# Longer turns on TensorE: sixteen pairs of sums, then half a batch of weighing

## The chip, the cores and the metric

The kernel runs on one core of a Trainium2 chip. The metric is the device time of one execution in microseconds (us); several executions are made and their median is taken. A core has engines that run side by side and wait for each other through semaphores: TensorE (PE in the profile, with its weight loads as PEld), VectorE (DVE), ScalarE (ACT), GpSimd (POOL, idle here) and SyncE (SP), which issues the transfers. TensorE writes only into PSUM, eight banks of 512 words in each of 128 partitions; ScalarE and VectorE bring results from there into the working memory, which the kernel holds as one large tensor called `arena`.

## The reference

The input `r_x` has 512 samples of 39 fields of 64 numbers. Two layers are computed, each a weighted sum over products of pairs of fields, and both are summed over the last axis:

```
h = x                               # (512, 39, 64)
for W in (W0, W1):                  # (39, 39, 128), (39, 128, 128)
    h = einsum('bid,bjd,ijh->bhd', x, h, W)
    outs.append(h)
y = concatenate(outs, axis=1).sum(axis=-1)      # (512, 256)
```

## The kernel before

The kernel doesn't build the first layer for each sample. It folds W0 and W1 into one table of coefficients, `c0`, with 115 slots of 128 columns, and then needs for each sample only sums over the 64 numbers of products of fields. The program has three stretches.

In the first two (TensorE at L381 and L402, ScalarE at L340, VectorE at L325) the table is made. In the third, from about 103 us to the end, the samples go through. They come in **pairs** (two samples in two halves of the partitions, 256 pairs in all), four pairs make a **group**, two groups a **unit**, and four units, that is eight groups, a **batch** of 32 pairs. There are eight batches.

In this stretch each engine has its own loop in a fixed order:

- VectorE makes the products of fields for a unit (`products`, L282 to L295) into a ring of four units, once TensorE is done with the unit that lay there (semaphore `filled`).
- TensorE makes the sums of a group in `sums` (L425): 16 matmuls with a stationary operand of 64x32 and 230 columns. Eight of them, on two halves of the rows and four strips of 32 columns, can be in the array together. Since the numbers are fp32, each matmul stands in the trace as two passes, so that a group has 32 and a unit 64. A group fills a **couple** of PSUM banks. There are three couples, taken in turn (`couple(g)` is `g % 3` after the first batch), and `sums` waits on the semaphore `emptied` until the group that last used its couple has been copied out.
- ScalarE copies a group out of its couple with four copies (L360) into the sums of the batch, `s0`, of which there are two, and then counts `emptied` up.
- TensorE weighs a batch in `weigh` (L446): 115 matmuls, one for each slot, with the 64 sums of the slot as stationary operand and 128 columns of the table moving. They go in pairs on the two halves of the columns. The last part also has eleven matmuls at L454 and four at L460, and then `batch_done` is counted up. Weighing of a batch is spread over the sums of the batch that follows. The last batch is weighed by itself at the end.
- ScalarE takes a weighed batch out of PSUM at L347, before the first group of a later batch; VectorE adds its halves at L302. SyncE loads the fields (L205), moves four rows of sums across partitions when a batch has been copied out (`gather`, L241), and stores results (L246).

The four units of the first batch are summed amid the second stretch; 28 units remain for the loop on TensorE that the change rewrites:

```
for u in range(BATCH_UNITS, UNITS):
    n, turn = divmod(u, BATCH_UNITS)
    sums(2 * u)
    sums(2 * u + 1)
    weigh(n - 1, turn)
```

Here `weigh(n, turn)` does the slots from `each * turn`, with `each` 29: a quarter of the table's 115.

Of the kernel before, what the change touches and what calls it, by code (L numbers as in the profile page):

```python
# [21 lines left out]
SLOTS = 115  # L22
# [60 lines left out]
def cin_kernel(nc: bass.Bass, x: bass.AP, u_list: bass.AP, w1: bass.AP, v_first: bass.AP, v_second: bass.AP,  # L83
# [9 lines left out]
    BATCH_UNITS = PAIRS // UNIT  # L93
    UNITS = ALL_PAIRS // UNIT
    GROUPS = ALL_PAIRS // GROUP
    BATCH_GROUPS = PAIRS // GROUP
# [9 lines left out]
    IN_BANK = BANK // HID  # L106
    MIXED = (SLOTS + IN_BANK - 1) // IN_BANK
    CROSS = COPY1

    ctx = ExitStack()  # L110
    with ctx:
# [7 lines left out]
        def take(words):  # L119
            at = used[0]  # L120
            used[0] += words
            assert used[0] <= WORDS
            return at
# [12 lines left out]
        w0_t2_0 = take(4 * HID)  # L136
        c1_x0 = take(CROSS * HID)
        t2_0 = take(2 * 4 * B)
# [8 lines left out]
        c1_x_second0 = w0_t2_second0 + 4 * HID  # L147
        assert c1_x_second0 + CROSS * HID <= s0[1]
        w1_0 = s0[1]
# [33 lines left out]
        def mixed_bank(k):  # L183
            return k if k < 8 else k % 4
# [18 lines left out]
        def _(sp):  # L203
# [22 lines left out]
            sp.dma_start(view(w0_t2_second0, (1, 4 * HID)), w0_t2[1]).then_inc(out1_loaded, 16)  # L226
            sp.dma_start(view(c1_x0, (1, CROSS * HID)), c1_x[0]).then_inc(out1_loaded, 16)
            sp.dma_start(view(c1_x_second0, (1, CROSS * HID)), c1_x[1]).then_inc(out1_loaded, 16)
            for u in range(BATCH_UNITS, X_RING):
# [33 lines left out]
        def _(dve):  # L263
# [44 lines left out]
            dve.wait_ge(out1_loaded, 64)  # L308
            for at, second, words in ((w0_t2_0, w0_t2_second0, 4 * HID), (c1_x0, c1_x_second0, CROSS * HID)):
                w = view(at, (1, words))  # L310
# [58 lines left out]
        @block.tensor  # L369
        def _(pe):  # L370
            for i in range(DIRECT):
                if i >= 4:
                    pe.wait_ge(direct_copied, i - 3)
                for k in range(8 * i, 8 * i + 8):
                    piece, at = divmod(k, PIECE)
                    if at == 0:
                        pe.wait_ge(w1_loaded[piece], 16)
                    for c in range(4):
                        if k == 0 and c < 2:
                            pe.wait_ge(u_ready, c + 1)  # L380
                        done = nc.tensor.matmul(  # L381
                            bank_view((i % 4 * 2 + k % 8 // 4) * BANK + k % 4, (4, SLOTS),
                                      rows=(ROWS * c, ROWS * c + ROWS)),
                            view(w1_0 + piece * PLACES * PIECE + ROW0[c % 2] * PIECE + at, (PIECE, ROWS)),
                            view(u0 + c % 2 * LIST + c // 2 * SLOTS, (1, SLOTS)), start=True, stop=True)
                done.then_inc(direct_filled, 1)

            def mixed(k):
                bank = mixed_bank(k)
                if k < 8:  # L390
                    pe.wait_ge(direct_copied, DIRECT - 4 + k // 2 + 1)
                else:
                    pe.wait_ge(c_added, k - 8 + 1 if k < 12 else k - 4 + 1)
                first = [True] * 4
                for j in range(IN_BANK * k, min(IN_BANK * k + IN_BANK, SLOTS)):
                    of = [terms(c % 2, PAIR_OF[c][j]) for c in range(4)]
                    for t in range(2):
                        for c in range(4):
                            if t >= len(of[c]):
                                continue  # L400
                            row, m = of[c][t]
                            done = nc.tensor.matmul(  # L402
                                bank_view(bank * BANK + j % IN_BANK * HID, (1, HID), rows=(ROWS * c, ROWS * c + ROWS)),
                                view(v0 + row * ROWS, (1, ROWS)), view(w1_0 + m * PIECE, (PLACES * PIECE, PIECES), (1, PIECE)),
                                start=first[c], stop=True, skip_group_check=True)
                            first[c] = False
                done.then_inc(mixed_filled, 1)

            def sums(g):
                u, turn = divmod(g, 2)  # L410
                before = last_user(g)
                if before is not None:
                    pe.wait_ge(emptied, before + 1)
                else:
                    pe.wait_ge(c_added, COUPLES[couple(g)] + 2 if g < BATCH_GROUPS else MIXED)
                if turn == 0:
                    pe.wait_ge(prod_ready, u + 1)
                for m in range(2):
                    for odd in range(2):
                        pair = GROUP * turn + 2 * odd + m  # L420
                        for r in range(2):
                            rows = (HALF * r, HALF * r + HALF)
                            for which in range(2):
                                c = 2 * odd + which
                                done = nc.tensor.matmul(  # L425
                                    bank_view((COUPLES[couple(g)] + r) * BANK + m, (2, LIST),
                                              rows=(ROWS * c, ROWS * c + ROWS)),
                                    view(x0 + u % X_RING * XU + pair * X_WORDS + X_MAIN + ROW0[which], (1, ROWS), rows=rows),
                                    view(prod0 + u % PROD_RING * PROD + pair * 2 * LIST + which * LIST, (1, LIST), rows=rows),
                                    start=True, stop=True)  # L430
                done.then_inc(filled, 1)

            def weigh(n, turn):
                at = (2 + n % 2) * BANK
                if turn == 0:
                    pe.wait_ge(emptied, BATCH_GROUPS * (n + 1))
                    if n == 0:
                        pe.wait_ge(c_added, MIXED)
                    if n >= 2:
                        pe.wait_ge(out_ready, n - 1)  # L440
                each = -(-SLOTS // BATCH_UNITS)
                for j in range(each * turn, min(each * turn + each, SLOTS)):
                    side = j % 2
                    rows = (HALF * side, HALF * side + HALF)
                    sums_of = view(s0[n % 2] + j * B, (1, B))
                    nc.tensor.matmul(bank_view(at + HID, (1, HID), rows=rows), sums_of, view(c0 + j * HID, (1, HID)),  # L446
                                     start=j < 2, stop=True, skip_group_check=True)
                if turn < BATCH_UNITS - 1:
                    return
                if n == 0:  # L450
                    pe.wait_ge(out1_ready, 2)
                for j in range(CROSS):
                    side = j % 2
                    nc.tensor.matmul(bank_view(at, (1, HID), rows=(HALF * side, HALF * side + HALF)),  # L454
                                     view(s0[n % 2] + j * B, (1, B)), view(c1_x0 + j * HID, (1, HID)),
                                     start=False, stop=True, skip_group_check=True)
                pe.wait_ge(t2_moved[n % 2], 64 * (n // 2 + 1))
                for c in range(4):
                    side = 1 - c % 2
                    done = nc.tensor.matmul(bank_view(at, (1, HID), rows=(HALF * side, HALF * side + HALF)),  # L460
                                            view(t2_0 + (4 * (n % 2) + c) * B, (1, B), rows=(0, SLOTS)),
                                            view(w0_t2_0 + c * HID, (1, HID), rows=(0, SLOTS)),
                                            start=False, stop=True, skip_group_check=True)
                done.then_inc(batch_done, 1)

            pe.wait_ge(v_ready, 1)
            for k in range(MIXED):
                mixed(k)
                if k in SUMS_BEHIND:
                    sums(2 * SUMS_BEHIND[k])  # L470
                    sums(2 * SUMS_BEHIND[k] + 1)
            for u in range(BATCH_UNITS, UNITS):
                n, turn = divmod(u, BATCH_UNITS)
                sums(2 * u)
                sums(2 * u + 1)
                weigh(n - 1, turn)
            for turn in range(BATCH_UNITS):
                weigh(BATCHES - 1, turn)


# [90 lines left out]
```

## Time and profile before

| | |
|---|---|
| median of three runs | 275.45 us (273.75 to 276.93) |
| profiled execution | 277.26 us, of which its span 275.5 us |
| granted TensorE clock over the span | 0.994 |
| TensorE busy | 258.4 us (94%) |
| VectorE, ScalarE busy | 173.6 us, 156.3 us |

The span goes from the first instruction to the last; the execution's own time has 1.8 us more around it. A TensorE record is a pass of a matmul, with an end that is modelled, so the distance from start to start tells more than the length of one. A weight load (PEld) belongs to each pass. "L425" is line 425 of the kernel as printed above. In a row of the timeline, brackets say how long the engine was idle before it and what released it; "issue" means that the profile shows nothing it waited for.

### The profile page before, as it was taken

The page shows a single profiled execution, that of the slowest core. Times are in us where ns is not written, and L with a number is a line of the kernel's source. Part 1 is how long each engine was busy: PE and PEld are TensorE (multiplying, and loading weights), DVE is VectorE, ACT ScalarE, POOL GpSimd, SP SyncE. Part 2 cuts the span into 40 slices and gives each one's busy share as a digit, 9 for nine tenths or more (in the row PEclk, how much of TensorE's full clock was granted, in tenths as well). Part 3 has the DMA queues.
Part 4 walks back from the last instruction along what each step waited for, and adds up shares of the span by engine and source line. Part 5 has one row for each costly group of instructions (what it writes and reads, how often), then busy time and mean ns, then how long its engine had stood idle before and what let it go on. Part 6 is the DMA issues. An engine that isn't in the chain of part 4 may idle for free.

```text
span 275.5 us, 14507 instructions
## 1 busy us (share of the span) xinstructions
PE 258.4 (94%) x6842; PEld 232.8 (85%) x6842; DVE 173.6 (63%) x333; ACT 156.3 (57%) x281; POOL 0.2 (0%) x4
## 2 busy tenths in 40 slices
PE   0977789999999999999999999999999999999995
PEld 0967789998999978888888888888888888888994
DVE  1009996733397699996887986996898689200000
ACT  1242344004164267887787887877887788778300
POOL 0000000000000000000000000000000000000000
PEclk9997999999999999999999999999999999999999
DMA  6999200001011012222132222322231220100100
GB/s 220 356 406 413 82 2 5 6 5 49 5 51 45 11 52 66 68 79 66 51 91 67 63 61 62 98 59 58 66 99 50 69 58 2 29 5 2 29 2 10
DMA packets 11019, 20.78 MB, mean 75 GB/s; under 512 B 4816, under 2 KB 5584, under 8 KB 10704
## 3 DMA queue, kind: packets, MB, share of 16 engines
q1 hardware_dynamic: 10960, 19.87, 23.3%
q8 instruction: 53, 0.87, 1.3%
q14 instruction: 6, 0.05, 0.1%
HBM read 18.40 MB, written 0.52 MB: 69 GB/s over the span
## 4 chain that ended last, share of the span: by engine, by line
PE 94%; issue 2%; DMA 2%; DVE 0%; SPq 0%; ACT 0%
PE psum L446 39%; PE psum L425 20%; PE psum L402 18%; PE psum L381 12%; PE psum L454 3%; DMA arena<-in_w 2%; PE psum L460 2%; SPq L213 0%; DVE arena L325 0%; DVE arena L302 0%; ACT arena L347 0%
## 5 line engine op out<-in xcount | busy, mean ns | idle before, releaser
L360 ACT COPY arena<-psum 64x460 f32<-64x460 f32 x256 | 137.3, 536 | 63.2 <-PE psum L425 60.1
L446 PEld LDWEIGHTS psum<-arena 128*64 128x64 f32 x1840 | 102.3, 137 | 10.3 <-issue 10.3
L446 PE MATMUL psum<-arena 128*64 128x128 f32 x1840 | 109.3, 274 | 0.0
L284 DVE TENSOR_TENSOR arena<-arena 128x1600 f32<-128x1600 f32 x32 | 58.2, 1820 | 0.1
L425 PE MATMUL psum<-arena 64*32 64x230 f32 x2048 | 57.5, 357 | 0.7 <-DVE arena L325 0.7
L402 PE MATMUL psum<-arena 128*32 128x128 f32 x1690 | 50.5, 274 | 0.2
L402 PEld LDWEIGHTS psum<-arena 128*32 128x32 f32 x1690 | 48.2, 109 | 2.7 <-issue 2.7
L425 PEld LDWEIGHTS psum<-arena 64*32 64x32 f32 x2048 | 38.1, 106 | 11.7 <-issue 5.6
L381 PE MATMUL psum<-arena 128*32 128x115 f32 x1024 | 32.3, 289 | 13.0 <-DMA arena<-in_w 6.9
L381 PEld LDWEIGHTS psum<-arena 128*32 128x32 f32 x1024 | 30.6, 163 | 14.5 <-issue 7.6
L325 DVE TENSOR_TENSOR arena<-arena,psum 128x512 f32<-128x512 f32 (+1 forms) x29 | 19.3, 682 | 21.2 <-PE psum L402 21.1
L295 DVE TENSOR_TENSOR arena<-arena 128x800 f32<-128x800 f32 x32 | 31.6, 988 | 0.0
L340 ACT COPY arena<-psum 128x920 f32<-128x920 f32 x16 | 14.8, 926 | 29.4 <-PE psum L381 29.4
L293 DVE TENSOR_TENSOR arena<-arena 128x720 f32<-128x720 f32 x32 | 29.0, 905 | 0.0
L302 DVE TENSOR_TENSOR arena<-psum,arena 64x256 f32<-64x256 f32 x8 | 3.3, 412 | 36.4 <-ACT arena L347 36.4
L282 DVE COPY arena<-arena 128x72 f32<-128x72 f32 x32 | 6.3, 198 | 19.3 <-PE psum L425 19.3
L347 ACT COPY arena<-psum 64x256 f32<-64x256 f32 x8 | 2.9, 368 | 23.0 <-PE psum L460 23.0
L273 DVE TENSOR_TENSOR arena<-arena 128x3040 f32<-128x3040 f32 x1 | 3.3, 3326 | 16.3 <-DMA arena<-in_v_second 16.3
L454 PE MATMUL psum<-arena 128*64 128x128 f32 x176 | 12.0, 273 | 0.0
L454 PEld LDWEIGHTS psum<-arena 128*64 128x64 f32 x176 | 10.9, 137 | 0.0
L289 DVE TENSOR_TENSOR arena<-arena 128x128 f32<-128x128 f32 x32 | 9.2, 287 | 0.0
L287 DVE TENSOR_TENSOR arena<-arena 128x128 f32<-128x128 f32 x32 | 9.2, 287 | 0.0
(13 smaller groups left out, 41.8 us busy)
## 6 DMA issues: line engine op xcount, KB each, us to landing
arena<-in_x SPq DMA_DIRECT2D x32, 312.0 KB, 3.2
arena<-in_w SPq DMA_DIRECT2D x4, 640.0 KB, 5.7
arena<-in_v_first SPq DMA_DIRECT2D x1, 1520.0 KB, 8.8
arena<-in_v_second SPq DMA_DIRECT2D x1, 1520.0 KB, 12.1
arena<-in_c_x SPq DMA_DIRECT2D x2, 704.0 KB, 11.4
arena<-arena SPq DMA_DIRECT2D x32, 28.8 KB
arena<-in_w_t SPq DMA_DIRECT2D x2, 256.0 KB, 8.9
out<-arena SPq DMA_DIRECT2D x8, 64.0 KB, 2.8
```

The source lines that it names most:

```text
L284: mult(view(to + 20, TO, (10, 20), (1, 10)), view(main, T, (1, 20), (0, 10)), view(x, T, (1, 20), (1, 10)), ALU.mult)
L287: mult(view(to, TO, (8, 2), (1, 8)), view(x + X_N1, T, (0, 2), (1, 8)), view(x + X_N1, T, (2, 2), (1, 8)), ALU.mult)
L293: mult(view(second + 25, TO, (10, 9), (1, 10)), view(half, T, (1, 9), (0, 10)), view(half, T, (1, 9), (1, 10)), ALU.mult)
L295: mult(view(second + 130, TO, (10, 10), (1, 10)), view(half + 9, T, (1, 10), (0, 10)), view(half + 9, T, (1, 10), (1, 10)), ALU.mult).then ...
L325: add(c, c, bank_view(mixed_bank(k) * BANK, (1, words)), ALU.add).then_inc(c_added, 1)
L340: nc.scalar.copy(view(c0 + 8 * i, (4, 2), (HID, SLOTS), (1, 4)), bank_view(i % 4 * 2 * BANK, (BANK, 2), (4, SLOTS), (1, 4))).then_inc(dire ...
L360: done = nc.scalar.copy(view(s0[n % 2] + 8 * in_batch + 4 * odd, (B, SLOTS), (2, 2), (1, 2), rows=(HALF * q, HALF * q + HALF)), bank_view( ...
L381: done = nc.tensor.matmul(bank_view((i % 4 * 2 + k % 8 // 4) * BANK + k % 4, (4, SLOTS), rows=(ROWS * c, ROWS * c + ROWS)), view(w1_0 + pi ...
L402: done = nc.tensor.matmul(bank_view(bank * BANK + j % IN_BANK * HID, (1, HID), rows=(ROWS * c, ROWS * c + ROWS)), view(v0 + row * ROWS, (1 ...
L425: done = nc.tensor.matmul(bank_view((COUPLES[couple(g)] + r) * BANK + m, (2, LIST), rows=(ROWS * c, ROWS * c + ROWS)), view(x0 + u % X_RIN ...
L446: nc.tensor.matmul(bank_view(at + HID, (1, HID), rows=rows), sums_of, view(c0 + j * HID, (1, HID)), start=j < 2, stop=True, skip_group_che ...
L454: nc.tensor.matmul(bank_view(at, (1, HID), rows=(HALF * side, HALF * side + HALF)), view(s0[n % 2] + j * B, (1, B)), view(c1_x0 + j * HID, ...
```

## The change

The loop over units becomes a loop over groups. After every fourth group, in place of every second, a part of the weighing follows, and the parts are halves (`TURNS` is 2, `each` becomes 58) in place of quarters. Every matmul, copy, product and transfer remains, with the same semaphores; only TensorE's order changes. The other engines' programs are the same.

```
+    TURN = 4
+    TURNS = BATCH_GROUPS // TURN
...
-                each = -(-SLOTS // BATCH_UNITS)
+                each = -(-SLOTS // TURNS)
...
-                if turn < BATCH_UNITS - 1:
+                if turn < TURNS - 1:
                     return
...
-            for u in range(BATCH_UNITS, UNITS):
-                n, turn = divmod(u, BATCH_UNITS)
-                sums(2 * u)
-                sums(2 * u + 1)
-                weigh(n - 1, turn)
-            for turn in range(BATCH_UNITS):
+            for g in range(BATCH_GROUPS, GROUPS):
+                n, in_batch = divmod(g, BATCH_GROUPS)
+                sums(g)
+                if in_batch % TURN == TURN - 1:
+                    weigh(n - 1, in_batch // TURN)
+            for turn in range(TURNS):
                 weigh(BATCHES - 1, turn)
```

TensorE's order at the start of the third stretch, before. One group is a row with its waits and the row of fifteen behind it; L446 is the weighing.

```order
L425 MATMUL psum<-arena 32x230 [waits prod_ready,c_added]
L425 MATMUL psum<-arena 32x230 x15
L425 MATMUL psum<-arena 32x230 [waits emptied]
L425 MATMUL psum<-arena 32x230 x15
L446 MATMUL psum<-arena 64x128 [waits c_added,emptied]
L446 MATMUL psum<-arena 64x128 x28
L425 MATMUL psum<-arena 32x230 [waits prod_ready,emptied]
```

Two groups, 29 weighings, and the next groups. The same place after the change, where line 425 has become 427 and 446 has become 448:

```order
L427 MATMUL psum<-arena 32x230 [waits prod_ready,c_added]
L427 MATMUL psum<-arena 32x230 x15
L427 MATMUL psum<-arena 32x230 [waits emptied]
L427 MATMUL psum<-arena 32x230 x15
L427 MATMUL psum<-arena 32x230 [waits prod_ready,emptied]
L427 MATMUL psum<-arena 32x230 x15
L427 MATMUL psum<-arena 32x230 [waits emptied]
L427 MATMUL psum<-arena 32x230 x15
L448 MATMUL psum<-arena 64x128 [waits c_added,emptied]
L448 MATMUL psum<-arena 64x128 x57
```

The third and fourth group moved ahead of the first weighing. With three couples the fourth group waits for the copies of the first, and no weighing stands between them any more.

## Rows read from the trace of the kernel before

**Rows 1.** The page: busy us, share of the span, instructions of each engine.

```profile
PE 258.4 (94%) x6842; PEld 232.8 (85%) x6842; DVE 173.6 (63%) x333; ACT 156.3 (57%) x281; POOL 0.2 (0%) x4
```

**Rows 2.** The chain that ended last, in order of time: start us, us, what.

```profile
152.59 1.72 PE psum L425 x64
154.30 3.42 PE psum L446 x58
157.72 1.71 PE psum L425 x64
...
167.78 1.09 PE psum L454 x20
...
257.82 12.56 PE psum L446 x228
```

**Rows 3.** Windows, PEld alone: stretch, its us, busy us (loads), clock, DMA share, GB/s.

```profile
163.00:164.16 1.17, 1.01 (x48) 1.00 0.00 0
```

**Rows 4.** Timeline, all engines, one unit: start us, us, engine, line, what, idle before.

```profile
162.78 1.35 PEld L425 LDWEIGHTS psum<-arena 64*32 64x32 f32 x64 [0.17 <-issue]
162.78 1.78 PE L425 MATMUL psum<-arena 64*32 64x230 f32 x64
...
163.90 4.39 ACT L360 COPY arena<-psum 64x460 f32<-64x460 f32 x8 [0.75 <-PE psum L425]
164.50 3.04 PEld L446 LDWEIGHTS psum<-arena 128*64 128x64 f32 x56 [0.37 <-issue]
...
169.45 1.35 PEld L425 LDWEIGHTS psum<-arena 64*32 64x32 f32 x64 [0.17 <-issue]
...
169.56 0.37 ACT L347 COPY arena<-psum 64x256 f32<-64x256 f32 x1 [1.28 <-PE psum L460]
```

**Rows 5.** Timeline, ACT alone, cut to the first group of that unit.

```profile
163.90 2.18 ACT L360 COPY arena<-psum 64x460 f32<-64x460 f32 x4 [0.75 <-PE psum L425]
```

**Rows 6.** Line 360: duration ns min/median/max, first and last start us.

```profile
L360 ACT COPY arena<-psum x256: 533/537/540, 65.6 to 256.0; 64x460 f32<-64x460 f32 x128
```

**Rows 7.** The chain again, where TensorE waits for VectorE.

```profile
102.62 0.56 DVE arena L325
103.18 0.04 issue
103.23 1.79 PE psum L425 x64
```

**Rows 8.** Windows, all engines: us, PE, PEld, DVE, ACT, POOL busy (instructions), clock, DMA, GB/s.

```profile
160.00:180.00 20.00, 20.00 (x462) 17.68 (x464) 16.77 (x34) 16.23 (x31) 0.00 (x0) 1.00 0.29 76
```

**Rows 9.** Waits: line, whom it waited for: us in total, times, longest us.

```profile
DVE arena L282 <- PE psum L425: 19.3, 20, 2.2
```

**Rows 10.** Timeline, SyncE: the gather of a batch and the load behind it.

```profile
168.31 2.91 SPq L241 DMA_DIRECT2D arena<-arena  x4
171.34 0.57 SPq L205 DMA_DIRECT2D arena<-in_x  x1
```

**Rows 11.** Windows on TensorE's pauses in the first stretch; columns as in Rows 8.

```profile
15.47:16.30 0.83, 0.01 (x1) 0.00 (x0) 0.00 (x0) 0.19 (x1) 0.00 (x0) 1.00 1.08 454
16.30:19.80 3.50, 3.50 (x127) 3.27 (x128) 0.00 (x0) 1.68 (x2) 0.00 (x0) 1.00 0.96 397
19.80:22.47 2.67, 0.00 (x1) 0.00 (x0) 1.52 (x1) 0.17 (x1) 0.00 (x0) 1.00 1.04 402
22.47:27.58 5.11, 5.11 (x128) 4.89 (x128) 5.11 (x9) 1.61 (x2) 0.00 (x0) 0.67 1.03 415
27.58:28.40 0.82, 0.00 (x1) 0.00 (x1) 0.82 (x2) 0.24 (x1) 0.00 (x0) 1.00 0.88 348
28.40:31.88 3.48, 3.48 (x128) 3.26 (x127) 3.48 (x9) 1.65 (x2) 0.00 (x0) 1.00 0.20 74
```

## The prediction

> **What bounds the kernel now.** I read the page's list of engines first. TensorE is busy for 258.4 us of the 275.5 us span, VectorE for 173.6 and ScalarE for 156.3 [rows 1]. Such shares are averages over three different stretches, so the second view is the chain of work that ended last, in order of time. From 103 us on it shows nothing but TensorE: 64 passes of sums in 1.72 us, 58 passes of weighing in 3.42 us, and the next sums directly behind, at 157.72 [rows 2]. The reader is to see that no wait stands between these pieces, so in this stretch only TensorE's own time counts, and that a unit takes 157.72 - 152.59 = 5.13 us. The 28 units of the loop all have this form (the last of each batch has L454 and L460 besides).
>
> The third view is the timeline of one such unit with all engines. It shows two things that the chain hides: small gaps on TensorE's weight loads, 0.17 us before the sums and 0.37 us before the weighing, both put down to "issue" [rows 4], and how ScalarE is paced. Its first copy begins 163.90 - 162.78 = 1.12 us after the unit's first pass, the eight copies of two groups take 4.39 us, and then it is idle for 0.75 us until the next unit [rows 4]. ScalarE is thus not the bound, but it is not far from it.
>
> **What a change of work costs TensorE.** This is what the change removes. The price follows from the pace within each kind of work. In the middle of the sums 48 loads lie in a window of 1.17 us [rows 3], which is six waves of eight (eight matmuls share the array), 0.195 us for a wave. A unit's 64 passes are eight waves, 1.56 us. For the weighing, the 20 passes at L454, which have the same shape, take 1.09 us [rows 2], 54.5 ns for a pass; the long row at the end gives 12.56/228 = 55.1 ns with its start in it. So 58 passes would take 3.16 us (3.20 by the other row). A unit without changes of work would take 4.72 us, and it takes 5.13: a round trip, sums to weighing and back, costs 0.41 us (0.37 by the other row). The two gaps of the weight loads add up to 0.54 us and lie at exactly these two places [rows 4]; part of them is a pass's ordinary spacing, so 0.45 is my upper end, and 0.30 the lower.
>
> Before there are 28 round trips in the loop, after it 14. **Saved: 14 x 0.41 = 5.7 us**, all on the path that sets the end, since TensorE has no wait there that could swallow it.
>
> **What the new order adds: a wait for ScalarE.** The wait itself is in the code of both kernels: a group may fill its couple only when the group three before it has been copied out. Before, two groups were followed by 3.42 us of weighing, in which ScalarE caught up. Now four groups follow each other, and the fourth needs the couple of the first. Take T as the first pass of the first group.
>
> - A group is four waves, 0.78 us. The fourth group would begin after twelve, at T + 2.34, some 0.02 us later for the first wave.
> - ScalarE begins at T + 1.12 and its four copies of the first group take 2.18 us [rows 5], to T + 3.30. That their time depends on what TensorE does meanwhile is not to be seen: all 256 copies lie between 533 and 540 ns, in the second stretch as in the third [rows 6].
> - The release: where TensorE waited for VectorE, 0.04 us lie between the end of that engine's work and the first pass [rows 7]; I take 0.05. TensorE goes on at T + 3.35.
>
> The wait is 3.35 - 2.36 = 0.99 us, and the restart adds the slower first wave again, **1.0 us for each of the 14 halves, 14.0 us**. The bounds: with no release time and the start of the copies 0.03 us sooner it is 0.9; with a release of 0.2 us, well above any row, 1.15. In the first half of all the fourth group is number 11, whose couple was last used by group 8, so that it waits as well.
>
> Behind the waiting instruction stand the 16 matmuls of the fourth group and then the half of the weighing, all of TensorE's work; nothing covers the wait. No second wait grows out of it. With the 1.0 us the fourth group ends near T + 4.2. A half then lasts two units plus 0.59 us, 10.26 + 0.59 = 10.85 us. ScalarE begins at T + 1.12 and has four groups at 2.2 us, so it is done at T + 9.9, about 0.9 us before the next half starts. Its couples are free then, so that only the fourth group waits. The copy at L347, which it makes between batches, starts 0.1 us after the next unit's first pass and takes 0.37 us [rows 4], less than the 1.12 us it has.
>
> **Other engines, at nothing.** VectorE's busy share in the steady stretch is 16.77 us in 20 [rows 8], and it waited for TensorE to free a place of its ring 20 times [rows 9]: it runs ahead. The second unit of a half is now read 2.6 us sooner after the first, but the ring holds four units, and two are always ready when a half begins, since VectorE gets 10.85 us for two units that keep it busy for some 8.6 (16.77/20 of 10.26 us). SyncE's gather of a batch waits for ScalarE's last copy, is issued in 2.91 us [rows 10] and is needed only at the end of the next batch; the load behind it waits for a unit that TensorE reaches after the next half has begun. These are free. If the cover of VectorE went, it would show as a wait of L425 for VectorE, and each would be worth at most the excess of two units' products over a half, which is negative here.
>
> **The sum.** 14 x (1.0 - 0.41) = 8.3 us, with bounds of 14 x (0.9 - 0.45) = 6.3 and 14 x (1.15 - 0.30) = 11.9. The profiled execution took 277.26 us, 1.8 us above the median and a little above the highest of the three runs, so it would go to 285.5 (span 283.8). Against the median of 275.45 the forecast is **283.7 us**, 3.0% slower.
>
> **The rivals.**
>
> *The clock falls in the new pauses (slower still).* In the first stretch TensorE pauses several times. After 2.67 us without work the granted clock over the next block is 0.67 on average, between the two levels of 1.2 and 2.4 GHz, and the block takes 5.11 us where its neighbour takes 3.50 [rows 11]. If each half met this, it would cost 14 x 1.6 = 22.5 us more: 306 us. Against it: pauses of 0.83 and 0.82 us, about as long as the one I forecast (0.99 less the run of the last passes), are followed by 1.00 [rows 11]. The Trainium skill, in "TensorE: Matmul & The Clock Gate", section "A second HAM failure mode: psum-queue depth-cycling", describes just this, an engine that idles briefly between groups as it cycles through PSUM banks and drops to the half clock. By that rule 306 would be the likely end. The rows on short pauses speak against it here. Chance 4%.
>
> *The fourth group does not wait (faster).* If ScalarE handed the first couple back by T + 2.36, only the saving would remain: 275.45 - 5.7 = 269.7 us. The point from which it decides is a wait of 0.41 us, a couple back by T + 2.77. The four copies would have to take 1.6 us in place of 2.18, or begin 0.6 us sooner, in the middle of the first group's own waves. The narrow spread of the copies speaks against it [rows 6]. For it speaks only that TensorE's ends are modelled, and I have no row in which it waits at this place. Chance 7%.
>
> *The saving is not there (slower).* If the 0.41 us belonged to the groups or to the semaphores and not to changes of work, the wait alone would remain: 275.45 + 14.0 = 289.5 us. Against it: the window of six waves lies across the border of two groups, with its wait, and keeps its pace [rows 3]. Chance 5%.
>
> *Wait and saving cancel (no change).* This needs a wait between 0.2 and 0.6 us, 272.5 to 278; no row gives a duration of that size. Chance 4%.
>
> **How the numbers follow.** The forecast's own case has the remaining 80%. Its bounds give 281.8 to 287.3 us; a median of few runs may lie some 1 us off, as the runs of before do, but the ends of the bounds are less likely than the middle. The range of 281.5 to 287.0 leaves out the rivals on both sides. Time differences under 1% are what a measurement of this kernel can hardly tell from no change, 2.75 us. Slower by over 1%: 80 + 4 + 5 = 89%. Faster: 7%. Within: 4%.
>
> **What the changed profile would show.** Once in each half a wait of L427 for ScalarE's L362, 14 in all, each 0.85 to 1.0 us long, before the fourth group; the weight loads' gaps before L448 about 14 in place of 28; ScalarE idle once in a half, for about 2.0 us (0.9 before the half starts and 1.12 after); halves of 10.85 us (the second of a batch near 12.4); the clock at 1.00. I am wrong if these waits are missing or under 0.4 us, if a second group waits too, or if the clock falls.

## The result, and the profile after

The changed kernel takes 284.44 us in the median of four runs (284.25 to 284.86), the kernel before 275.64 in the four runs that it is compared with: a ratio of 1.031 (95% interval 1.026 to 1.037). It is slower by 8.8 us, where 8.3 was forecast, and 284.44 stands against a forecast of 283.7.

The page of the changed kernel, busy us by engine and the chain by engine:

```profile
PE 254.9 (90%) x6842; PEld 231.7 (82%) x6842; DVE 172.5 (61%) x333; ACT 156.3 (55%) x281; POOL 0.2 (0%) x4
...
PE 83%; ACT 11%; issue 3%; DMA 2%; DVE 0%; SPq 0%
```

No engine has more to do than in [rows 1]. What is new is ScalarE on the chain, with 11% of the span, 30 us: the stretches of the chain in which the end hangs on its copies and no longer on TensorE. That is more than was lost, because TensorE works on the second and third group meanwhile. The wait itself is in the waits of the changed kernel (line, whom it waited for: us, times, longest):

```profile
PEld psum L427 <- ACT arena L362: 17.1, 14, 1.2
...
PE psum L427 <- ACT arena L362: 11.0, 14, 0.8
...
PEld psum L448 <- issue: 5.2, 14, 0.4
```

The waits of the kernel before have, for the gaps before the weighing:

```profile
PEld psum L446 <- issue: 10.3, 28, 0.4
```

So TensorE waits for ScalarE fourteen times, once in each half, and the gaps of the loads before the weighing are 14 in place of 28. A wait is 1.2 us between weight loads and 0.8 us between matmuls, whose ends are modelled; neither is its cost, which the experiments take from the length of a half. One batch of the timeline, loads alone, shows where:

```profile
148.27 2.12 PEld L427 LDWEIGHTS psum<-arena 64*32 64x32 f32 x96 [0.17 <-issue]
151.62 0.57 PEld L427 LDWEIGHTS psum<-arena 64*32 64x32 f32 x32 [1.22 <-ACT arena L362]
152.56 6.31 PEld L448 LDWEIGHTS psum<-arena 128*64 128x64 f32 x116 [0.37 <-issue]
159.04 2.12 PEld L427 LDWEIGHTS psum<-arena 64*32 64x32 f32 x96 [0.17 <-issue]
162.39 0.57 PEld L427 LDWEIGHTS psum<-arena 64*32 64x32 f32 x32 [1.22 <-ACT arena L362]
...
171.56 0.54 PEld L427 LDWEIGHTS psum<-arena 64*32 64x32 f32 x28 [0.17 <-issue]
```

Three groups (96 loads) go through, then the fourth stands until 151.62 - 148.27 = 3.35 us after the first pass, which is the forecast moment to a hundredth. ScalarE in the same stretch:

```profile
149.39 8.80 ACT L362 COPY arena<-psum 64x460 f32<-64x460 f32 x16 [0.64 <-PE psum L427]
160.16 8.79 ACT L362 COPY arena<-psum 64x460 f32<-64x460 f32 x16 [1.98 <-PE psum L427]
```

It begins 1.12 us after the first pass, does four groups in a row and is then idle for 1.98 us within a batch: it is the slower of the two while sums are made, and the faster over a half. The halves take 159.04 - 148.27 = 10.77 and 171.56 - 159.04 = 12.52 us, a batch 23.29 us. In the chain of before a batch is 147.45 - 125.38 = 22.07 us:

```profile
125.38 1.71 PE psum L425 x64
...
147.45 1.71 PE psum L425 x64
```

Seven batches of 1.22 us make 8.5 us. The spans of the two profiled executions differ by only 7.0, because the loop of the changed kernel began sooner, at 101.69 us in its chain against 103.23 [rows 7]. That start moves between 101 and 105 us from execution to execution, after stretches of the program that the change leaves alone, so below the batch is compared before the total.

The clock did not fall (window over that batch; columns as in [rows 8]); over the whole loop, from 101.7 to 272 us, it is 1.00 as well:

```profile
148.00:172.00 24.00, 22.43 (x540) 19.59 (x545) 17.98 (x37) 17.86 (x34) 0.00 (x0) 1.00 0.25 65
```

### The profile page after: what moved, and what is told of

Its sections match the earlier page's. It is cut to its first block, busy times and chain, and to the rows that moved or that the text cites. A ratio compares the mean times of both kernels' runs of the same rounds, so it can differ in the third digit from the quotient of the medians.

```text
span 282.5 us, 14507 instructions
## 1 busy us (share of the span) xinstructions
PE 254.9 (90%) x6842; PEld 231.7 (82%) x6842; DVE 172.5 (61%) x333; ACT 156.3 (55%) x281; POOL 0.2 (0%) x4
## 4 chain that ended last, share of the span: by engine, by line
PE 83%; ACT 11%; issue 3%; DMA 2%; DVE 0%; SPq 0%
PE psum L448 36%; PE psum L404 17%; PE psum L427 13%; PE psum L383 11%; ACT arena L362 11%; PE psum L456 3%; DMA arena<-in_w 2%; PE psum L462 2%; SPq L215 0%; DVE arena L327 0%; DVE arena L304 0%; ACT arena L349 0%
## 5 line engine op out<-in xcount | busy, mean ns | idle before, releaser
L448 PE MATMUL psum<-arena 128*64 128x128 f32 x1840 | 104.7, 273 | 0.0
L427 PE MATMUL psum<-arena 64*32 64x230 f32 x2048 | 57.4, 357 | 11.7 <-ACT arena L362 11.0
L404 PE MATMUL psum<-arena 128*32 128x128 f32 x1690 | 49.6, 274 | 0.0
L456 PE MATMUL psum<-arena 128*64 128x128 f32 x176 | 13.5, 275 | 0.0
```

The lines of the kernel that those rows point to most:

```text
L404: done = nc.tensor.matmul(bank_view(bank * BANK + j % IN_BANK * HID, (1, HID), rows=(ROWS * c, ROWS * c + ROWS)), view(v0 + row * ROWS, (1 ...
L427: done = nc.tensor.matmul(bank_view((COUPLES[couple(g)] + r) * BANK + m, (2, LIST), rows=(ROWS * c, ROWS * c + ROWS)), view(x0 + u % X_RIN ...
```

## The experiments

The theory: the loss is a wait of 1.0 us for the first group's couple in each of 14 halves, less 0.41 us for each of 14 round trips between the two kinds of work. The main rivals: the saving isn't there, or the pause is TensorE's own. Later a third question came up, what the 0.41 us consists of.

**The couple given back sooner.** Of the first group of a half, ScalarE makes two copies in place of four, from batch 2 on.

```
-                for odd in range(2):
+                for odd in range(1 if g % 4 == 0 and g >= 16 else 2):
```

Expected: 

> The changed order, but ScalarE makes only two of the four copies of the first group of a half, in the 12 halves of batches 2 to 7 (the other half of that group's sums is not brought out, so this part of the computation is left out). The couple is then back about 1.1 us sooner, at T + 2.26, before the fourth group wants it at T + 2.36. Theory (the loss is the wait for that couple, 1.0 us a half, and the saving is 0.41 us for each of 14 round trips): the wait goes in 12 halves and stays in 2, 275.6 - 5.7 + 2.0 = 271.9 us. Rival 'the saving is not there': 275.6 + 2.0 = 277.6. Rival 'the pause before the fourth group is TensorE's own and not ScalarE's': no change from 284.4.

Measured: 273.44 us, 0.984 of before (0.979 to 0.990), which was 277.27 in these rounds. So 3.8 us are gained against before, where the theory had 275.6 - 271.9 = 3.7. The chain in a batch of this kernel:

```profile
127.44 3.27 PE psum L427 x128
...
137.19 3.27 PE psum L427 x128
140.46 6.37 PE psum L448 x113
...
148.68 3.27 PE psum L427 x128
```

The four groups are one piece with no wait. The first half takes 9.75 us in place of 10.77, so the wait cost 1.02 us. A batch takes 148.68 - 127.44 = 21.24 us, 0.83 less than before: this is the saving by itself, 0.41 us for each of the two round trips that went. Both rivals fall: there is a saving, and the pause goes when ScalarE is sooner.

**The control.** The same copies left out in the order of before.

Expected: 

> The order of before with the same copies left out (part of the sums of 12 groups is not brought out). A control: by the theory ScalarE is not on the path there, so 275.6 us, within 0.5%. If the copies cost TensorE something by themselves (shared PSUM), it would be faster by some us.

Measured: 275.32 us in one run, a little below the runs of before in the same rounds (276.60 to 279.63). The reason is the start of its loop, at 101.28 us, 1.95 sooner than in the profile before, which took 277.26. Its batch is unchanged, 145.50 - 123.43 = 22.07 us:

```profile
101.28 1.79 PE psum L425 x64
...
123.43 1.72 PE psum L425 x64
...
145.50 1.72 PE psum L425 x64
```

So these copies of ScalarE cost TensorE nothing where nobody waits for them.

**Half the dose.** Three copies of four.

```
-                    for q in range(2):
+                    for q in range(1 if g % 4 == 0 and g >= 16 and odd else 2):
```

Expected: 

> The changed order, with three of the four copies of the first group of a half, in the 12 halves of batches 2 to 7 (a quarter of that group's sums is not brought out). The couple is back one copy, 0.55 us, sooner. Theory: each of these 12 waits shrinks from 1.0 to 0.45 us, 284.4 - 12 x 0.55 = 277.8 us, between the full copies and the half copies. A fixed pause that is there or not would give 284.4 or the 273.4 of the half copies.

Measured: 278.72 us in one run, where 277.8 was expected. Loads alone, one half:

```profile
126.05 2.12 PEld L427 LDWEIGHTS psum<-arena 64*32 64x32 f32 x96 [0.17 <-issue]
128.85 0.57 PEld L427 LDWEIGHTS psum<-arena 64*32 64x32 f32 x32 [0.68 <-ACT arena L362]
...
136.28 2.12 PEld L427 LDWEIGHTS psum<-arena 64*32 64x32 f32 x96 [0.17 <-issue]
```

The fourth group goes on 2.80 us after the first pass, 0.55 sooner, and the half takes 10.23 us, between 10.77 and 9.75. The wait follows the copies one to one.

**Longer turns.** Eight groups, then a whole batch of weighing (`TURN = 8`).

Expected: 

> Eight groups in a row, then a whole batch of weighing: 7 round trips in place of 14. Theory: from the fourth group on TensorE goes at ScalarE's pace; group k begins at T + 1.12 + 2.2 (k - 2) + 0.05, the eighth at T + 12.2. A batch takes 12.2 + 0.8 + 260 passes at 54.5 ns (14.2) + 0.4 = 27.5 us against 22.07 before, so 275.6 + 7 x 5.4 = 313.6 us. Rival 'a turn costs one fixed pause': 7 x 1.0 - 21 x 0.41, 274 us. If the clock falls in the pauses of some 1.4 us each, over 320 us and a granted clock below 1.00 in the rows.

Measured: 321.56 us in one run: the theory's batch, and on top of it the fall of the clock that the expectation names last. The timeline of TensorE in a batch at full clock, with its first pass at 189.01:

```profile
189.01 2.56 PE L427 MATMUL psum<-arena 64*32 64x230 f32 x96
192.36 1.01 PE L427 MATMUL psum<-arena 64*32 64x230 f32 x32 [0.79 <-ACT arena L362]
...
201.19 1.01 PE L427 MATMUL psum<-arena 64*32 64x230 f32 x32 [1.20 <-ACT arena L362]
...
216.69 0.62 PE L427 MATMUL psum<-arena 64*32 64x230 f32 x16
```

The last row is the start of the next batch. From the fourth group on TensorE goes at ScalarE's 2.2 us a group, the eighth begins at T + 12.18, and the batch takes 27.68 us, where 27.5 was expected: five waits, not a fixed price for a turn. In five of the seven batches the same pauses bring the clock down. Windows on one of these, which begins at 130.86, and on the batch above (columns as in [rows 8]):

```profile
130.80:138.60 7.80, 4.65 (x162) 2.88 (x160) 5.78 (x13) 6.81 (x14) 0.00 (x0) 0.97 0.30 84
138.60:144.70 6.10, 5.23 (x96) 2.02 (x96) 6.10 (x15) 5.95 (x12) 0.00 (x0) 0.50 0.22 66
...
189.00:202.00 13.00, 7.43 (x257) 4.39 (x256) 11.03 (x22) 11.94 (x23) 0.00 (x0) 1.00 0.29 81
```

There the clock falls within the third pause (they are 0.8, 1.2 and 1.2 us) and stands at 0.50, the 1.2 GHz level, until the weighing. In the batch at 189 it stays at 1.00 with pauses just as long. The fall costs little in this order, since ScalarE sets the pace of the groups: a batch takes up to 29.6 us (159.40 to 189.01, where the low clock lasted into the weighing), but the first one, at 0.87 over its groups, takes the same 27.68 us as the one at full clock. By the lengths of the batches it is some 5 us of the 321.56 in all. The rival of the falling clock was thus no idle fear; in the changed kernel, with one pause of 0.8 us in a half, it stayed away.

**Shorter turns.** Single groups with an eighth of the weighing (`TURN = 1`).

Expected: 

> One group of sums, then an eighth of a batch of weighing (15 slots, the last 10): 56 round trips in place of 28, and no wait for ScalarE. Theory (a round trip costs 0.41 us wherever it stands): 275.6 + 28 x 0.41 = 287.1 us, with weight-load gaps of 0.37 and 0.17 us 56 times each. Rival 'the 0.41 us belongs to groups or semaphores, whose number is the same': 275.6.

Measured: 289.84 us in one run, against 277.27. The chain:

```profile
115.55 0.94 PE psum L427 x32
116.48 1.89 PE psum L448 x30
118.37 0.94 PE psum L427 x32
```

A group with its weighing takes 2.82 us, where half a unit took 2.57. Seven of them and a last one of 3.93 are 23.7 us a batch, 1.67 more than before for four more round trips: 0.42 each. Seven batches make 11.7 us, where 11.5 was expected. Without any wait the price is still there, so it belongs to the changes between kinds of work. But in the half copies a half of 58 weighings showed another price: 9.75 us less sixteen waves (3.12) and 116 passes at 54.5 ns (6.32) leave 0.31.

**Runs as long as the couples.** Three, three and two groups.

```
-    TURN = 4
-    TURNS = BATCH_GROUPS // TURN
+    RUN_ENDS = [2, 5, 7]
+    PARTS = [0, 43, 86, SLOTS]
+    TURNS = len(RUN_ENDS)
...
-                if in_batch % TURN == TURN - 1:
-                    weigh(n - 1, in_batch // TURN)
+                if in_batch in RUN_ENDS:
+                    weigh(n - 1, RUN_ENDS.index(in_batch))
```

Expected: 

> Runs of three, three and two groups of sums, with 43, 43 and 29 slots of weighing behind them: as many groups in a row as there are couples. Theory: no wait for ScalarE; 21 round trips in place of 28, at 0.41 us each, 2.9 us less than before (1.0%). If a round trip's price hangs on the number of matmuls (the traces so far give 0.31 us where 58 were weighed and 0.42 where 15 or 29 were, odd numbers), the three odd parts here cost 0.42, 0.42 and 0.53 us a batch, and the gain is 2.2 us (0.8%). If more than two groups in a row wait after all, slower than before.

Measured: 274.42 us, 0.995 of before (0.991 to 0.998). The chain:

```profile
124.02 2.49 PE psum L428 x96
...
145.78 2.49 PE psum L428 x96
```

No wait, and a batch takes 21.76 us, 0.31 less than before. Seven of these are 2.2 us, the smaller of the two expectations, in which odd parts cost more: 43 is odd. The total fell by 1.5 us, with an interval of 0.5 to 2.5 us.

**Even parts, in the order of before.** Quarters of 30, 30, 28 and 27 slots, and the halves of the columns swapped in the last fifteen matmuls of a batch.

```
+    PARTS = [0, 30, 60, 88, SLOTS]
...
-                    side = j % 2
+                    side = 1 - j % 2
...
-                    side = 1 - c % 2
+                    side = c % 2
```

Expected: 

> The order of before, with quarters of 30, 30, 28 and 27 slots in place of 29, 29, 29 and 28, and the halves of the columns swapped in the last fifteen matmuls of a batch, so that neighbours always lie on different halves. Theory 'part of the 0.41 us is a matmul without a partner at the end of an odd part': 0.31 us in place of 0.42 for each of 28 round trips, 2.9 us less than before (1.0%). Rival 'the whole 0.41 us is the change of work': no difference.

Measured: 272.86 us, 0.986 of before (0.981 to 0.991). The chain:

```profile
146.08 1.71 PE psum L426 x64
...
151.22 1.72 PE psum L426 x64
...
156.36 1.72 PE psum L426 x64
...
161.29 1.71 PE psum L426 x64
...
167.74 1.71 PE psum L426 x64
```

A unit with 30 weighings takes 5.14 us, as one with 29 did [rows 2]; with 28 it takes 4.93. So a pair of weighings on the two halves of the columns has a place of some 0.21 us, and a matmul whose neighbour lies on the same half takes a whole place. A batch is 21.66 us, 0.41 less than before, with every change of work still there: a quarter of the 0.41 us per round trip was not the change of work.

**The same swap in the changed order.**

Expected: 

> The changed order with the halves of the columns swapped in the last fifteen matmuls of a batch alone. Theory: the second half of a batch, whose 57 slots end on the half of the columns on which the eleven matmuls behind them begin, loses two unpaired places, 12.51 us to 12.3, and nothing else changes; the waits stay at 1.0 us. 7 x 0.2 = 1.5 us less than the changed kernel, some 283 us. Rival 'the longer second half comes from ScalarE's copy between batches': 12.51 us stays.

Measured: 286.21 us in one run, some 3 us more than expected. Its loop began late, at 105.34 us, 3.65 us after that of the changed kernel's profile (284.25 us), so the total by itself says little; less these 3.65 us it would be 282.6. Its loads show the expected second half, 12.30 us (139.20 to 151.50) in place of 12.52, and the first half and the wait unchanged; so it is the halves of the columns that count, as the number of matmuls is the same:

```profile
128.43 2.12 PEld L427 LDWEIGHTS psum<-arena 64*32 64x32 f32 x96 [0.17 <-issue]
131.77 0.57 PEld L427 LDWEIGHTS psum<-arena 64*32 64x32 f32 x32 [1.22 <-ACT arena L362]
...
139.20 2.12 PEld L427 LDWEIGHTS psum<-arena 64*32 64x32 f32 x96 [0.17 <-issue]
...
151.50 2.12 PEld L427 LDWEIGHTS psum<-arena 64*32 64x32 f32 x96 [0.17 <-issue]
```

**VectorE takes two of the four copies.** In the changed order, for the first group of each half, with a semaphore of its own for TensorE and SyncE to wait on.

```
+            def help_out(g):
...
+                dve.wait_ge(filled, g + 1)
...
+                    done = nc.vector.tensor_copy(
...
+                if u % 2 == 0 and u >= 2 * BATCH_UNITS:
+                    help_out(2 * (u - BATCH_UNITS))
                 products(u)
```

Expected: 

> The changed order, with nothing left out: VectorE makes two of the four copies of the first group of each half, beside ScalarE's two, placed ahead of the products that it makes then. Theory: the couple is back at about T + 2.3 and the wait is gone or under 0.2 us in 14 halves, 284.4 - 14 = 270.4 us, up to 273; 2% faster than before. Rival 'VectorE becomes the bound': its 18.3 us a batch grow by four copies of 0.5 to 0.7 us, to some 20.7, against a batch of 21.3; if its products come late, waits of L427 for VectorE show and the time stays at 275 or above.

Measured: 281.36 us, 1.018 of before (1.015 to 1.022). The theory's figure failed, and the time is above 275, as the rival has it. But what comes late is VectorE's copies and not its products, for none of which TensorE waits. The waits, and a first half and the half behind it in the timeline:

```profile
PE psum L454 <- DVE arena L324: 6.4, 6, 3.2
...
127.63 2.12 PEld L454 LDWEIGHTS psum<-arena 64*32 64x32 f32 x96 [0.17 <-issue]
...
128.81 1.29 DVE L324 COPY arena<-psum 64x460 f32<-64x460 f32 x2 [1.63 <-PE psum L454]
...
130.22 0.60 PEld L454 LDWEIGHTS psum<-arena 64*32 64x32 f32 x32 [0.47 <-ACT arena L387]
...
137.68 2.12 PEld L454 LDWEIGHTS psum<-arena 64*32 64x32 f32 x96 [0.17 <-issue]
...
139.44 1.29 DVE L324 COPY arena<-psum 64x460 f32<-64x460 f32 x2
...
140.85 0.60 PEld L454 LDWEIGHTS psum<-arena 64*32 64x32 f32 x32 [1.05 <-ACT arena L387]
```

In the first half VectorE waits for the group, and the fourth group goes on at T + 2.59, not 3.35; the half takes 10.05 us. In the second half VectorE is still at the products that stand before the copies in its program. It copies without idling before, until 140.73; the fourth group goes on at T + 3.17, 0.12 us later than that end. (The row names ScalarE's line for the wait, though ScalarE had long given its part.) A batch takes 22.42 us (127.63 to 150.05), better than 23.29 and worse than 22.07. The first half of all took 13.2 us (102.62 to 115.83), since the copies there stand behind the products of a unit, and TensorE waited up to 3.2 us for them. A copy by VectorE takes 640 ns, by ScalarE 537.

**Both gains together.** Runs of three, three and two, parts of 44, 44 and 27 slots (the last is even with the fifteen matmuls behind it) and the swap.

Expected: 

> Both things that gained, together and with nothing left out: runs of three, three and two groups, with 44, 44 and 27 slots behind them, and the halves of the columns swapped in the last fifteen matmuls. Theory: no wait for ScalarE, and three round trips a batch at 0.31 us. A batch takes 32 waves (6.22) + 260 passes at 54.5 ns (14.18) + 3 x 0.31 = 21.33 us against 22.07 before, 7 x 0.74 = 5.2 us less, 1.9% faster than before. If the two gains were one and the same, no better than the even quarters alone (21.65 us a batch, 1.1 to 1.4% faster).

Measured: 270.99 us, 0.979 of before (0.974 to 0.985). The chain:

```profile
122.47 2.49 PE psum L428 x96
...
143.81 2.49 PE psum L428 x96
```

A batch takes 21.34 us, as worked out. It is the fastest version with nothing left out: about 2% faster than before and some 5% faster than the change (0.979/1.031 = 0.950).

## Why the prediction was right

**The bound.** It held that TensorE alone sets the pace of the third stretch of before. Two runs show it: half of ScalarE's copies of some groups were left out with no effect on a batch, and even parts, which spare TensorE four matmuls without a partner at 0.1 us each, shortened a batch by 0.41 us.

**The wait.** It was to stand before the fourth group of each half, 14 times, and to be 1.0 us. It is there 14 times, ends at T + 3.35 as worked out from ScalarE's start, its four copies and 0.05 us of release, and costs 1.02 us by the half copies. The row that was forecast for it, 0.85 to 1.0 us, came out as 1.2 between loads and 0.8 between matmuls; the cost lies between the two. It shrinks by a copy's time when a copy is left out.

**The saving.** 0.41 us for a round trip was right as a mean (0.41 by the half copies, 0.42 by the shorter turns), but the step that called all of it a change of work was wrong. It priced 58 passes at 54.5 ns each, 3.16 us, and this holds only where every matmul has a partner: 29 weighings take the time of 30. A round trip costs 0.31 us, and 0.1 us was an odd number of weighings, whose last matmul has no partner on the other half of the columns. That 14 x 0.41 came out even so is luck. Quarters of 29 always paid for a matmul without a partner, four times in a batch with the last part; the change's first half of 58 doesn't, and its second half of 57, with the eleven matmuls behind it, pays twice. So this cost fell by half, as the number of round trips did. The halves came out at 10.77 and 12.52 us, where 10.85 and 12.4 were forecast, and the errors cancel within a batch, 1.22 us against 2 x 0.59 = 1.18.

**What was priced at nothing.** The copies between batches, SyncE's gather and VectorE show no wait in TensorE's rows of the changed kernel. One figure was misread without harm: the second unit of a half is read 5.13 - 1.6 = 3.5 us sooner after the first, not 2.6, since the wait comes only before its second group. VectorE was called ahead, and it is, but by less than it seemed: with two copies more in each half it came late.

**The rivals.** That the fourth group does not wait, and that wait and saving cancel, are refuted by the waits; that the saving is missing by the half copies, which are faster than before. The clock stayed at 1.00 in the changed kernel, with one pause of 0.8 us in a half, but the rival's mechanism exists: it fell to 0.50 in five of the seven whole batches, where the groups from the fourth on stood behind pauses of 0.8 to 1.2 us. The Trainium skill, in "TensorE: Matmul & The Clock Gate", section "A second HAM failure mode: psum-queue depth-cycling", tells of a kernel whose TensorE idles briefly and often between groups and whose clock goes back and forth between its two levels. The trace of the whole batches agrees, with 0.50 and 1.00 in turn; that of the changed kernel shows no such fall, at 1.00 throughout its loop.

What stays open is why the start of the loop moves by some 4 us between executions of the same first two stretches; no run here varied it. Most of it is there when the first sums begin, at 62.2 us in the control and 65.8 us in the late run.

## What to carry to other kernels

When work is put into longer turns, count how many pieces the producer can make in a row before it has to wait for the consumer to give a buffer back: with three buffers a run of three was free and a run of four cost a wait longer than the saving. Take the price of a change of work from the trace by setting the piece's time against the pace in its middle, and look at what else has the same count; here a quarter of it was an odd number of matmuls. An engine that shows idle time in the mean may still be late at the one moment where help is wanted.

## What the hardware showed beyond that

Two matmuls of 64 columns on different halves of the array share a place of 0.218 us (four passes at 54.5 ns each). One without a partner takes the whole place: 29 and 30 weighings took the same 5.13 to 5.14 us with their sums, and 28 took 0.21 us less. In the whole-batch order the same run of pauses (0.8 us, then 1.2 us before each further group) brought the clock to 0.50 in five of seven batches, at or right behind the second, third or fourth pause, and left it at 1.00 in two.
